# Three streamed cross-attentions: the query stack and the mask row move to ScalarE's DMA queue, and the rows of ones are copied from a row in memory

## The chip, the cores and the metric

The kernel runs on one core of one Trainium2 chip. The metric is device time in microseconds (us) of that core, from one launch that does the whole forward pass. A core has five engines with an instruction stream each: TensorE (PE; its weight loads are listed as PEld), VectorE (DVE), ScalarE (ACT), GpSimd (POOL) and SyncE (SP). Copies between memory (HBM) and the on-chip buffers are made by 16 DMA engines, which work off what the streams issue. In the kernel before, every one of the program's copies is issued by SP.

## The reference

A perceiver of four layers over 128 latent tokens of width 256. Each layer has a cross-attention to a context of 12544 keys of width 192, a self-attention of some kind, and a feed-forward network of eight experts. For layers 0 to 2 the cross-attention is, cut to what matters:

```python
q = split_heads(layernorm(x) @ Wq + bq)          # 16 heads of 16, 128 queries
k = split_heads(ctx @ Wk + bk)                   # 12544 keys
v = split_heads(ctx @ Wv + bv)
s = einsum('bhid,bhjd->bhij', q, k) / 4          # layer 0: keys outside the mask get -inf
x = x + merge(softmax(s) @ v) @ Wo + bo
```

## The kernel before, in words

`build` runs stages one after the other, each in a `Stage` with a barrier behind it: `setup`, `project_context`, then per layer a cross-attention, its output, a self-attention and the experts. `project_context` computes keys and values of layers 0 to 2 once; keys are written to memory (`key_parts`) as three bf16 parts whose sum is the fp32 key, values to `values_scratch`.

`streamed_cross_attention(layer)` (line 410) runs for layers 0, 1 and 2; in layer 1 it is called by `guarded_cross_attention`. Its fp32-like product of query and key is one matmul over stacked bf16 parts: rows 0 to 95 of the tile `keys` hold six copies of key parts of one head (6 times 16), and rows 0 to 95 of `q_stack` the query parts that go with them. Three further rows of `keys` (96 to 98) hold ones; opposite them in `q_stack` GpSimd later puts the negated maximum of each query in three parts. In layer 0 a fourth row, 99, holds the mask (0 or a very large negative number), with a row of ones opposite in `q_stack`.

The 16 heads are streamed. A head has 7 chunks of 1792 keys; `keys` and `values` have room for DEEP = 3 heads. `fill(h, j)` issues the copies of two chunks of a head (one chunk for j = 3): 48, 32 and 16 rows of keys (line 476) and the values (line 479), four copies in all; this text calls it a fill group. From head 3 on, a fill group waits until the sums of the chunks it overwrites are done. Per chunk, PE makes the scores with queries as rows (`top`, line 549), DVE reduces them to a maximum (line 697), and when a head's maximum is known and in `q_stack`, PE makes the scores again with keys as rows (`scores`, line 560), ACT takes exp (line 610) and PE sums probabilities times values (`sums`, line 573). `top` runs LEAD = 10 chunks ahead of `scores`, so that for the first 10 chunks `top` runs alone.

At the start of such a stage the order of SP's stream is written out by hand: Wq, bias or mask, the rows of ones into `keys` (line 489), the four fill groups of head 0; in layer 0 then a wait for the mask row computed by DVE (`drop_bf`), its copy to memory (`mask_row`, line 496), a wait for that, and three copies from there into row 99 (line 500); then a wait for the query parts (`qparts`, DVE, line 690), three copies of them to memory (`query_parts`, line 505), a wait for those, six copies back into `q_stack` (line 511, 16 rows of 16 times 128 each), in layer 0 one more for its row of ones (line 515); then the fill groups of heads 1 and 2 and of the rest. PE's first `top` waits for all rows of ones and mask (`key_rows`), the whole stack (`stack`) and the first fill group.

The source of the ones is `ones_bf`, a tile of 128 by 128; the copy into `keys` reads three of its rows 294 times over:

```python
sp.dma_start(keys[SEG:SEG + 3, :, :].rearrange("p s (n t) -> p (s n) t", t=128),
             g.ones_bf[0:3, :].unsqueeze(1).to_broadcast([3, RING * TPC, 128]))\
```

Of the kernel before, what the change touches and what calls it, by code (L numbers as in the profile page):

```python
# [149 lines left out]
def setup(nc, g, a):  # L150

    with ExitStack() as ctx:
        st = Stage(nc, ctx, "setup")
        block = st.block()

        @block.sync
        def _(sp):
            sp.dma_start(g.x[:], a["x"].rearrange("b t d -> (b t) d")).then_inc(st.sem("x"), 16)
            sp.wait_ge(st.sem("x"), 16)

        @block.gpsimd
        def _(pool):
            pool.memset(g.band[:], 0.0).then_inc(st.sem("zeroed"), 1)
            pool.memset(g.minus_half[:], -0.5)
            pool.memset(g.zeros[:], 0.0)
            pool.wait_ge(st.sem("zeroed"), 1)

            pool.affine_select(out=g.band[:], in_=g.band[:], compare_op=ALU.not_equal, fill=1.0, base=-127,
                               pattern=[[1, 255]], channel_multiplier=-1).then_inc(st.sem("band"), 1)

        @block.vector
        def _(dve):
            dve.memset(g.ones[:], 1.0)
            dve.memset(g.ones_bf[:], 1.0)
            dve.wait_ge(st.sem("band"), 1)
            dve.tensor_copy(g.ident_bf[:], g.ident)

            dve.tensor_copy(g.sel[:], g.ident[:, 0:32]).then_inc(st.sem("sel"), 1)
            dve.wait_ge(st.sem("sel"), 1)
            for i in range(1, 4):  # L180
                dve.tensor_tensor(g.sel[:], g.sel[:], g.ident[:, 32 * i:32 * i + 32], ALU.add)\
                   .then_inc(st.sem("sel"), 1)
                dve.wait_ge(st.sem("sel"), i + 1)
# [226 lines left out]
def streamed_cross_attention(layer):  # L410
# [18 lines left out]
    def stage(nc, g, a):  # L429
        with ExitStack() as ctx:  # L430
# [37 lines left out]
            def _(sp):  # L468
# [17 lines left out]
                          .then_inc(sem("wq"), 16)  # L486
                if masked:
                    sp.dma_start(mask8[:], a["mask"].rearrange("(p n) -> p n", p=128)).then_inc(sem("mask"), 16)
                sp.dma_start(keys[SEG:SEG + 3, :, :].rearrange("p s (n t) -> p (s n) t", t=128),
                             g.ones_bf[0:3, :].unsqueeze(1).to_broadcast([3, RING * TPC, 128]))\  # L490
                  .then_inc(sem("key_rows"), 16)
                for j in range(len(PAIRS)):
                    fill(0, j)
                if masked:
                    sp.wait_ge(sem("drop"), 1)
                    sp.dma_start(dram(g.mask_row, 0, [[NK // 128, 128], [1, NK // 128]]), drop_bf[:])\
                      .then_inc(sem("mask"), 16)
                    sp.wait_ge(sem("mask"), 32)
                    for p in range(DEEP):
                        sp.dma_start(keys[SEG + 3:SEG + 4, p * NCH:p * NCH + NCH, :],  # L500
                                     dram(g.mask_row, 0, [[NK, 1], [CH, NCH], [1, CH]])).then_inc(sem("key_rows"), 16)

                sp.wait_ge(sem("qparts"), 1)
                for part in range(3):
                    sp.dma_start(dram(g.query_parts, part * D * T, [[T, 128], [128 * T, DG], [1, T]]),
                                 qparts[:, part, :, :]).then_inc(sem("qparts_out"), 16)
                sp.wait_ge(sem("qparts_out"), 48)
                for at, copies in ((0, 3), (3, 2), (5, 1)):
                    for part in range(copies):
                        src = dram(g.query_parts, part * D * T, [[T, HD], [HD * T, H], [1, T]])  # L510
                        sp.dma_start(q_stack[at * HD + part:(at + copies) * HD:copies, :, :], src)\
                          .then_inc(sem("stack"), 16)
                if masked:
                    sp.wait_ge(sem("stack_zero"), 1)
                    sp.dma_start(q_stack[SEG + 3:SEG + 4, :, :],
                                 g.ones_bf[0:1, :].unsqueeze(1).to_broadcast([1, H, T]))\
                      .then_inc(sem("stack"), 16)
                for h in range(1, H):
                    for j, (c, n) in enumerate(PAIRS):
                        if h >= DEEP:  # L520
                            sp.wait_ge(sem("sums"), (h - DEEP) * NCH + c + n)
                        fill(h, j)

            @block.tensor
            def _(pe):
# [10 lines left out]
                    pe.matmul(bank(g, 2, 0, 1), g.ones[:], some[:], start=True, stop=True)\  # L536
                      .then_inc(sem("mask_count"), 1)
                pe.wait_ge(sem("stack"), STACK)
                pe.wait_ge(sem("key_rows"), 16 * (1 + DEEP) if masked else 16)
                pe.wait_ge(sem("q"), 1)  # L540

                def top(v, w):
# [10 lines left out]
                def scores(k):  # L553
                    h = (k * GROUP + GROUP - 1) // (NCH * TPC)
                    pe.wait_ge(sem("shifted"), 4 * (h + 1))
                    at_least(pe, sem("probs"), k - 2)
                    for i in range(GROUP):
                        tile = k * GROUP + i
                        u, key = tile // TPC, tile % TPC * 128
                        last = pe.matmul(score_bank(k)[:, i * 128:i * 128 + 128], keys[0:P2, u % RING, key:key + 128],  # L560
                                         q_stack[0:P2, u // NCH, :], start=True, stop=True, skip_group_check=True)
                    last.then_inc(sem("scores"), 1)
# [41 lines left out]

            @block.scalar
            def _(act):
                def exp(k):
                    act.wait_ge(sem("scores"), k + 1)
                    at_least(act, sem("sums"), -(-(k * GROUP + GROUP - HELD) // TPC))
                    act.activation(group_probs(k), score_bank(k), ACT.Exp).then_inc(sem("probs"), 1)  # L610

                def copy_tiles(h):
                    act.wait_ge(sem("sums"), NCH * (h + 1))
                    act.copy(tiles[:, h, :], sum_bank).then_inc(sem("tiles"), 1)

                for u in range(NU):
                    k = (u * TPC + GROUP // 2) // GROUP
                    exp(k)
                    exp(k + 1)
                    exp(k + 2)  # L620
                    if u % 2 == 0:
                        exp(k + 3)
                    if u % NCH == 0 and u > 0:
                        copy_tiles(u // NCH - 1)
                copy_tiles(H - 1)
# [2155 lines left out]
def build(nc, a, out, stages=None):  # L2781
    with ExitStack() as ctx:
# [18 lines left out]
        g.values = nc.dram_tensor("values_scratch", (3, H, NCH, 128, TPC * VW), F32, kind="Internal").ap()  # L2801
        g.query_parts = nc.dram_tensor("query_parts", (3, D, T), BF16, kind="Internal").ap()
        g.mask_row = nc.dram_tensor("mask_row", (1, NK), BF16, kind="Internal").ap()
        g.acc, g.neg_all = sb("acc", [T, H, VW]), sb("neg_all", [T, H])
        run = {name for name in ORDER} if stages is None else set(stages)
        setup(nc, g, a)
# [69 lines left out]
```

## Time and profile before

| | us |
|---|---|
| median of 3 runs | 3386.88 |
| the 3 runs | 3374.2, 3387.84, 3386.88 |
| the profiled execution, its own time | 3375.52 |
| its span, first to last instruction | 3373.8 |
| busy: PE / DVE / ACT / POOL | 2941.7 / 1829.3 / 1349.5 / 405.4 |
| mean granted TensorE clock, share of full | 0.906 |

Busy times are those of the span; an engine's busy time counts neither its waits nor the issuing of copies. What a stage costs beyond its busy time stands in the idle times before instructions and in what ended them.

### The profile page before, as it was taken

What the parts mean: (1) busy time and instruction counts of PE and PEld (TensorE: products, weight loads), DVE (VectorE), ACT (ScalarE), POOL (GpSimd) and SP (SyncE); (2) the same over time, 40 slices, a digit from 0 to 9 for tenths busy, and PEclk for the clock granted to TensorE, in tenths of its full rate; (3) what the DMA queues carried; (4) which work ended last, traced back from release to release, by engine and by line L of the source; (5) the groups of instructions that cost most, each with busy time, mean ns of one, the idle gap of its engine ahead of it and who ended that gap; (6) DMA issues with size and microseconds to landing.
All of it is one profiled execution on the core that took longest, in us unless ns stands there. A gap on an engine that the chain in (4) does not pass through costs nothing. (4 is left out here: it accounts for less than half of the span.)

```text
span 3373.8 us, 66493 instructions
## 1 busy us (share of the span) xinstructions
PE 2941.7 (87%) x27158; PEld 2484.3 (74%) x27158; DVE 1829.3 (54%) x3246; ACT 1349.5 (40%) x2191; POOL 405.4 (12%) x571
## 2 busy tenths in 40 slices
PE   6878829998677999576999669999999999999978
PEld 6878725776474777473777455999999999999867
DVE  5445427774426775455776343555555555555524
ACT  4444314666003667122667120444344344444311
POOL 2333310000100000000000002220202020200000
PEclk9989968999787999686999685999999999999969
DMA  4877868883468884059885271201101010000016
GB/s 154 266 259 253 274 190 184 177 175 62 154 192 179 174 177 88 26 204 181 177 175 103 83 213 38 57 11 29 39 1 39 1 39 1 1 1 1 17 50 227
DMA packets 244901, 393.95 MB, mean 117 GB/s; under 512 B 33491, under 2 KB 207957, under 8 KB 244597
## 3 DMA queue, kind: packets, MB, share of 16 engines
q1 hardware_dynamic: 244599, 389.70, 44.9%
q8 instruction: 217, 3.56, 0.5%
q14 instruction: 85, 0.69, 0.1%
HBM read 289.45 MB, written 99.49 MB: 115 GB/s over the span
## 5 line engine op out<-in xcount | busy, mean ns | idle before, releaser
L697 DVE TENSOR_REDUCE L_xattn_tops<-psum 128x1 f32<-128x896 f32 x672 | 702.1, 1086 | 264.8 <-PE psum L549 263.6
L610 ACT ACTIVATE L_xattn_probs<-psum 128x512 f32<-128x512 f32 x1176 | 612.0, 600 | 489.4 <-PE psum L560 489.3
L1705 DVE TENSOR_TENSOR L_units_low<-psum,L_units_high 128x896 fp32r<-128x896 f32 x224 | 243.6, 1088 | 486.7 <-ACT L_units_high L1654 486.7
L549 PE MATMUL psum<-L_xattn_keys,L_xattn_q_stack 96*128 96x448 bf16 (+1 forms) x1344 | 393.6, 377 | 109.0 <-DMA L_xattn_q_stack<-query_parts 64.5
L1622 PE MATMUL psum<-wide_tokens,L_units_high 128*128 128x386 f32 x1568 | 456.4, 358 | 1.4 <-DVE L_units_low L1705 1.4
L560 PEld LDWEIGHTS psum<-L_xattn_q_stack,L_xattn_keys 99*128 99x128 bf16 (+1 forms) x4704 | 321.4, 98 | 143.3 <-issue 17.4
L560 PE MATMUL psum<-L_xattn_q_stack,L_xattn_keys 99*128 99x128 bf16 (+1 forms) x4704 | 392.4, 221 | 5.0 <-ACT L_xattn_probs L610 5.0
L1623 PE MATMUL psum<-wide_tokens,L_units_low 128*128 128x194 f32 x1568 | 395.1, 252 | 0.0
L573 PE MATMUL psum<-L_xattn_probs,L_xattn_values 128*17 128x128 f32 x9408 | 357.1, 276 | 0.0
L1654 ACT CAST L_units_high<-psum 128x896 fp32r<-128x896 f32 x224 | 203.3, 908 | 363.6 <-PE psum L1610 363.6
L1646 ACT ACTIVATE L_units_raw<-L_units_raw,L_units_negmax 128x896 f32<-128x896 f32 x224 | 221.6, 1037 | 307.9 <-DVE L_units_negmax L1696 307.9
L1623 PEld LDWEIGHTS psum<-wide_tokens,L_units_low 128*128 128x128 f32 x1568 | 299.1, 191 | 1.7
L1622 PEld LDWEIGHTS psum<-wide_tokens,L_units_high 128*128 128x128 f32 x1568 | 294.9, 188 | 3.0 <-DVE L_units_low L1705 1.6
L573 PEld LDWEIGHTS psum<-L_xattn_probs,L_xattn_values 128*17 128x17 f32 x9408 | 260.1, 98 | 38.0 <-ACT L_xattn_probs L610 0.6
L1686 DVE TENSOR_SCALAR_CACHE_REDUCE L_units_raw<-psum 128x448 f32<-128x448 f32 x448 | 259.8, 617 | 4.0 <-POOL wide_acc L1665 2.6
L549 PEld LDWEIGHTS psum<-L_xattn_keys,L_xattn_q_stack 96*128 96x128 bf16 (+1 forms) x1344 | 91.4, 99 | 219.1 <-issue 67.1
L1610 PE MATMUL psum<-band,L_units_raw 128*128 128x128 f32 x1568 | 207.9, 272 | 2.0 <-ACT L_units_raw L1646 2.0
L395 POOL TENSOR_TENSOR proj_parts<-proj_rest,proj_parts 128x896 bf16<-128x896 f32 x84 | 161.6, 1925 | 280.0 <-ACT proj_parts L313 280.0
L1610 PEld LDWEIGHTS psum<-band,L_units_raw 128*128 128x128 f32 x1568 | 179.9, 140 | 10.3 <-ACT L_units_raw L1646 2.4
L1598 PE MATMUL psum<-wide_high_a,wide_q_high 128*128 128x448 f32 x448 | 184.5, 412 | 2.2 <-PEq L78 2.2
L2563 PE MATMUL psum<-xnT,L_ffn_w 128*128 128x128 f32 x1056 | 141.6, 292 | 27.3 <-DMA L_ffn_w<-in_L_ffn_W 14.0
L2563 PEld LDWEIGHTS psum<-xnT,L_ffn_w 128*128 128x128 f32 x1056 | 137.3, 206 | 36.0 <-issue 14.0
(436 smaller groups left out, 3990.3 us busy)
## 6 DMA issues: line engine op xcount, KB each, us to landing
key_parts<-proj_parts SPq DMA_DIRECT2D x84, 672.0 KB, 4.1
L_xattn_keys<-key_parts SPq DMA_DIRECT2D x144, 336.0 KB, 4.7
values_scratch<-proj_values SPq DMA_DIRECT2D x21, 1904.0 KB, 17.4
L_xattn_values<-values_scratch SPq DMA_DIRECT2D x144, 238.0 KB, 5.2
L_ffn_w<-in_L_ffn_W SPq DMA_DIRECT2D x32, 1024.0 KB, 6.9
L_xattn_keys<-key_parts SPq DMA_DIRECT2D x144, 224.0 KB, 5.0
L_xattn_keys<-key_parts SPq DMA_DIRECT2D x192, 112.0 KB, 5.0
L_ffn_w<-in_L_ffn_w SPq DMA_DIRECT2D x16, 1024.0 KB, 6.4
```

The costliest lines, as they stand in the source:

```text
L549: last = pe.matmul(top_slot(n)[:, s, :], q_stack[0:P1, h, :], keys[0:P1, v % RING, key:key + WIN // 2], start=True, stop=True)
L560: last = pe.matmul(score_bank(k)[:, i * 128:i * 128 + 128], keys[0:P2, u % RING, key:key + 128], q_stack[0:P2, u // NCH, :], start=True, s ...
L573: last = pe.matmul(sum_bank[row:row + VW, :], values[:, u % RING, t, :], probs[:, at:at + 128], start=(c * TPC + t < 4), stop=(c * TPC + t ...
L610: act.activation(group_probs(k), score_bank(k), ACT.Exp).then_inc(sem("probs"), 1)
L697: dve.tensor_reduce(tops[:, h % 2, 2 * c + w:2 * c + w + 1], top_slot(n), AX.XY, ALU.max)\
L1610: last = pe.transpose(turned_banks(gr)[:, t * 128:t * 128 + 128], raw[u % 2][:, key:key + 128], g.ident)
L1622: pe.matmul(out, high[gr][:, cols], rhs, start=(tile == 0), stop=False, skip_group_check=True)
L1623: last = pe.matmul(out[:, 0:C + 2], low[gr][:, cols], rhs[:, 0:C + 2], start=False, stop=(tile == TPC - 1), skip_group_check=True)
L1646: act.activation(half, half, ACT.Exp, bias=new).then_inc(sem("probs"), 1)
L1686: dve.tensor_scalar(raw[u % 2][:, s * SUB:s * SUB + width], bank(g, s % 2, 0, width), 0.0, None, ALU.add, ALU.max, accum_out=tops[:, h, s: ...
L1705: dve.tensor_tensor(low[gr][:], turned_banks(gr), high[gr][:], ALU.subtract).then_inc(sem("low"), 1)
L2563: last = pe.matmul(bank(g, 2 * slot + half, j * T, j * T + T), buf[par][:, k, col:col + 128], g.xnT[:, k, :], start=(k == 0), stop=(k == D ...
```

## The change

In `setup`, one further copy writes the tile of ones to a new row in memory, `ones_row` of 12544 values. In the streamed attention, SP issues only Wq, bias or mask, and then all fill groups, head 0 to 15. ACT, before its first exp, issues the rows of ones (from `ones_row`, 3 times 21 pieces of 1792 values), in layer 0 the whole mask path and the stack's row of ones, then one copy of all query parts to memory instead of three, and the same six copies into `q_stack`. PE's wait for the rows of ones moves from the first `top` to the first `scores` in layers 1 and 2, and stays where it was in layer 0 (where the first `scores` waits too).

```diff
@@ setup @@
             sp.dma_start(g.x[:], a["x"].rearrange("b t d -> (b t) d")).then_inc(st.sem("x"), 16)
-            sp.wait_ge(st.sem("x"), 16)
+            sp.wait_ge(st.sem("ones_bf"), 1)
+            sp.dma_start(dram(g.ones_row, 0, [[128, NK // 128], [1, 128]]), g.ones_bf[0:NK // 128, :])\
+              .then_inc(st.sem("x"), 16)
+            sp.wait_ge(st.sem("x"), 32)
...
-            dve.memset(g.ones_bf[:], 1.0)
+            dve.memset(g.ones_bf[:], 1.0).then_inc(st.sem("ones_bf"), 1)
@@ streamed_cross_attention, sync @@
-                sp.dma_start(keys[SEG:SEG + 3, :, :].rearrange("p s (n t) -> p (s n) t", t=128),
-                             g.ones_bf[0:3, :].unsqueeze(1).to_broadcast([3, RING * TPC, 128]))\
-                  .then_inc(sem("key_rows"), 16)
-                for j in range(len(PAIRS)):
-                    fill(0, j)
-                if masked:
-                    sp.wait_ge(sem("drop"), 1)
...
-                sp.wait_ge(sem("qparts"), 1)
-                for part in range(3):
-                    sp.dma_start(dram(g.query_parts, part * D * T, [[T, 128], [128 * T, DG], [1, T]]),
-                                 qparts[:, part, :, :]).then_inc(sem("qparts_out"), 16)
-                sp.wait_ge(sem("qparts_out"), 48)
...
-                for h in range(1, H):
+                for h in range(H):
@@ tensor @@
-                pe.wait_ge(sem("key_rows"), 16 * (1 + DEEP) if masked else 16)
+                if masked:
+                    pe.wait_ge(sem("key_rows"), 16 * (1 + DEEP))
...
                 def scores(k):
                     h = (k * GROUP + GROUP - 1) // (NCH * TPC)
                     pe.wait_ge(sem("shifted"), 4 * (h + 1))
+                    if k == 0:
+                        pe.wait_ge(sem("key_rows"), 16 * (1 + DEEP) if masked else 16)
@@ scalar @@
+                act.dma_start(keys[SEG:SEG + 3, :, :], dram(g.ones_row, 0, [[0, 3], [0, RING], [1, CH]]))\
+                   .then_inc(sem("key_rows"), 16)
+                if masked:
+                    act.wait_ge(sem("drop"), 1)
+                    act.dma_start(dram(g.mask_row, 0, [[NK // 128, 128], [1, NK // 128]]), drop_bf[:])\
+                       .then_inc(sem("mask"), 16)
+                    act.wait_ge(sem("mask"), 32)
+                    for p in range(DEEP):
+                        act.dma_start(keys[SEG + 3:SEG + 4, p * NCH:p * NCH + NCH, :],
+                                      dram(g.mask_row, 0, [[NK, 1], [CH, NCH], [1, CH]])).then_inc(sem("key_rows"), 16)
+                    act.wait_ge(sem("stack_zero"), 1)
+                    act.dma_start(q_stack[SEG + 3:SEG + 4, :, :],
+                                  g.ones_bf[0:1, :].unsqueeze(1).to_broadcast([1, H, T]))\
+                       .then_inc(sem("stack"), 16)
+
+                act.wait_ge(sem("qparts"), 1)
+                act.dma_start(dram(g.query_parts, 0, [[T, 128], [D * T, 3], [128 * T, DG], [1, T]]), qparts[:])\
+                   .then_inc(sem("qparts_out"), 16)
+                act.wait_ge(sem("qparts_out"), 16)
+                for at, copies in ((0, 3), (3, 2), (5, 1)):
+                    for part in range(copies):
+                        src = dram(g.query_parts, part * D * T, [[T, HD], [HD * T, H], [1, T]])
+                        act.dma_start(q_stack[at * HD + part:(at + copies) * HD:copies, :, :], src)\
+                           .then_inc(sem("stack"), 16)
```

SP's stream before, at the start of layer 1's streamed attention (each fill group is four rows; the middle of head 0 is left out):

```order
L482 DMA L_xattn_wq<-in_L_xattn_Wq 128x2x256
L485 DMA L_xattn_bq<-in_L_xattn_bq 128x1 x2
L489 DMA L_xattn_keys<-ones_bf 3x294x128
L476 DMA L_xattn_keys<-key_parts 48x1x3584
...
L476 DMA L_xattn_keys<-key_parts 16x1792
L479 DMA L_xattn_values<-values_scratch 128x238
L505 DMA query_parts<-L_xattn_qparts 128x2x128 x3
L511 DMA L_xattn_q_stack<-query_parts 16x16x128 x6
L476 DMA L_xattn_keys<-key_parts 48x1x3584
```

The same place of SP's stream in the changed kernel (line numbers are its own, 3 higher here):

```order
L485 DMA L_xattn_wq<-in_L_xattn_Wq 128x2x256
L488 DMA L_xattn_bq<-in_L_xattn_bq 128x1 x2
L479 DMA L_xattn_keys<-key_parts 48x1x3584
...
L479 DMA L_xattn_keys<-key_parts 16x1792
L482 DMA L_xattn_values<-values_scratch 128x238
L479 DMA L_xattn_keys<-key_parts 48x1x3584
```

The ones and the query copies are gone from it, and head 1's first fill group follows head 0's last. ACT's stream in the changed kernel at the start of layer 0's streamed attention; before, the exps (line 610 then) were its first rows there:

```order
L584 DMA L_xattn_keys<-ones_row 3x21x1792
L588 DMA mask_row<-L_xattn_drop_bf 128x98
L592 DMA L_xattn_keys<-mask_row 1x12544 x3
L595 DMA L_xattn_q_stack<-ones_bf 1x16x128
L600 DMA query_parts<-L_xattn_qparts 128x6x128
L606 DMA L_xattn_q_stack<-query_parts 16x16x128 x6
L612 ACTIVATE L_xattn_probs<-psum 128x512 x28
```

In layers 1 and 2 the rows of lines 588, 592 and 595 are absent. The copies stand ahead of all exps of the stage, in the order in which they are needed.

## Rows read from the trace of the kernel before

**Rows 1.** Page: costliest groups, the one that carries the first wait.

```profile
L549 PE MATMUL psum<-L_xattn_keys,L_xattn_q_stack 96*128 96x448 bf16 (+1 forms) x1344 | 393.6, 377 | 109.0 <-DMA L_xattn_q_stack<-query_parts 64.5
```

**Rows 2.** Tile q_stack: who waited for it (engine, line: us, times).

```profile
  PEld psum L549: 100.0, 3
```

**Rows 3.** Timeline, layer 0's start: start us, us, engine, line, copy [idle before].

```profile
469.20 0.97 SPq L489 DMA_DIRECT2D L_xattn_keys<-ones_bf  x1
...
475.86 0.27 DVE L677 TENSOR_SCALAR L_xattn_drop_bf<-L_xattn_drop,L_xattn_any_key 128x98 bf16<-128x98 f32 x1
...
490.51 0.34 SPq L496 DMA_DIRECT2D mask_row<-L_xattn_drop_bf  x1
498.55 0.82 SPq L500 DMA_DIRECT2D L_xattn_keys<-mask_row  x3
499.42 1.41 SPq L505 DMA_DIRECT2D query_parts<-L_xattn_qparts  x3
504.43 3.85 SPq L511 DMA_DIRECT2D L_xattn_q_stack<-query_parts  x6
508.32 0.59 SPq L515 DMA_DIRECT2D L_xattn_q_stack<-ones_bf  x1
...
510.23 1.67 PE L549 MATMUL psum<-L_xattn_keys,L_xattn_q_stack 100*128 100x448 bf16 x4 [34.85 <-DMA L_xattn_q_stack<-ones_bf]
...
511.20 14.97 DVE L697 TENSOR_REDUCE L_xattn_tops<-psum 128x1 f32<-128x896 f32 x14 [32.15 <-PE psum L549]
```

**Rows 4.** Timeline, layer 1's start.

```profile
992.70 0.84 SPq L489 DMA_DIRECT2D L_xattn_keys<-ones_bf  x1
...
993.59 12.46 SPq L476 DMA_DIRECT2D L_xattn_keys<-key_parts  x3
...
998.72 0.43 DVE L690 TENSOR_TENSOR L_xattn_qparts<-L_xattn_qrest,L_xattn_qparts 128x256 bf16<-128x256 f32 x1
...
1006.55 1.84 SPq L476 DMA_DIRECT2D L_xattn_keys<-key_parts  x3
1008.43 0.42 SPq L479 DMA_DIRECT2D L_xattn_values<-values_scratch  x1
...
1013.57 1.46 SPq L505 DMA_DIRECT2D query_parts<-L_xattn_qparts  x3
1023.73 3.87 SPq L511 DMA_DIRECT2D L_xattn_q_stack<-query_parts  x6
...
1029.40 1.67 PE L549 MATMUL psum<-L_xattn_keys,L_xattn_q_stack 96*128 96x448 bf16 x4 [32.61 <-DMA L_xattn_q_stack<-query_parts]
```

**Rows 5.** Timeline, layer 2's start.

```profile
1514.27 0.42 DVE L690 TENSOR_TENSOR L_xattn_qparts<-L_xattn_qrest,L_xattn_qparts 128x256 bf16<-128x256 f32 x1
...
1544.20 1.67 PE L549 MATMUL psum<-L_xattn_keys,L_xattn_q_stack 96*128 96x448 bf16 x4 [31.86 <-DMA L_xattn_q_stack<-query_parts]
```

**Rows 6.** Windows: stretch, its us, busy by engine, PEclk, DMA share, GB/s.

```profile
994.00:996.00 2.00, 1.28 (x6) 1.28 (x7) 0.43 (x1) 0.00 (x0) 0.00 (x0) 0.50 0.18 18
1000.00:1002.00 2.00, 0.00 (x0) 0.00 (x0) 0.00 (x0) 0.00 (x0) 0.00 (x0) 0.50 0.16 19
504.40:508.30 3.90, 0.00 (x0) 0.00 (x0) 0.00 (x0) 0.00 (x0) 0.00 (x0) 0.50 0.30 67
514.00:530.00 16.00, 13.55 (x31) 2.00 (x30) 15.62 (x17) 0.00 (x0) 0.77 (x4) 0.50 1.06 207
```

**Rows 7.** DMA view, 499 to 504 us: GB/s in 40 equal slices.

```profile
GB/s 0 0 0 201 0 0 0 0 0 0 47 219 189 37 33 213 193 254 20 201 209 62 0 0 0 0 0 201 0 0 0 0 0 0 0 18 16 18 16 18
```

**Rows 8.** Page: issues by copy, KB each, median us to landing.

```profile
L_xattn_keys<-key_parts SPq DMA_DIRECT2D x144, 336.0 KB, 4.7
L_xattn_values<-values_scratch SPq DMA_DIRECT2D x144, 238.0 KB, 5.2
L_xattn_keys<-key_parts SPq DMA_DIRECT2D x144, 224.0 KB, 5.0
L_xattn_keys<-key_parts SPq DMA_DIRECT2D x192, 112.0 KB, 5.0
```

**Rows 9.** Tile query_parts, copies out and back: us to landing.

```profile
DMA to landing us min/median/max: 2.0/2.4/9.3
```

**Rows 10.** Timeline, the first 4 us: setup and the next stage's first copy.

```profile
0.81 0.41 SPq L158 DMA_DIRECT2D x<-in_x  x1
...
1.06 0.17 DVE L174 MEMSET ones_bf<- 128x128 bf16 x1
```

More of the change, by code:

```diff
@@ L488, in _ @@
                     sp.dma_start(mask8[:], a["mask"].rearrange("(p n) -> p n", p=128)).then_inc(sem("mask"), 16)
-                sp.dma_start(keys[SEG:SEG + 3, :, :].rearrange("p s (n t) -> p (s n) t", t=128),
-                             g.ones_bf[0:3, :].unsqueeze(1).to_broadcast([3, RING * TPC, 128]))\
-                  .then_inc(sem("key_rows"), 16)
-                for j in range(len(PAIRS)):
-                    fill(0, j)
-                if masked:
-                    sp.wait_ge(sem("drop"), 1)
[L496 to L501, printed above, removed]
-                sp.wait_ge(sem("qparts"), 1)
-                for part in range(3):
-                    sp.dma_start(dram(g.query_parts, part * D * T, [[T, 128], [128 * T, DG], [1, T]]),
-                                 qparts[:, part, :, :]).then_inc(sem("qparts_out"), 16)
-                sp.wait_ge(sem("qparts_out"), 48)
[L508 to L517, printed above, removed]
-                for h in range(1, H):
+                for h in range(H):
                     for j, (c, n) in enumerate(PAIRS):
@@ L2803, in build @@
         g.mask_row = nc.dram_tensor("mask_row", (1, NK), BF16, kind="Internal").ap()
+        g.ones_row = nc.dram_tensor("ones_row", (1, NK), BF16, kind="Internal").ap()
         g.acc, g.neg_all = sb("acc", [T, H, VW]), sb("neg_all", [T, H])
```

## The prediction

> **What bounds the kernel now.** I read the page's costliest groups first: TensorE's first score matmul of the streamed attention stood idle for copies, 64.5 us of it for the query stack [rows 1]. The view of the tile q_stack gives the whole: 100.0 us in 3 waits, one at the start of each of layers 0, 1 and 2 [rows 2]. That is 3% of the span and all that this change can reach, since behind the first matmul nothing of the program differs.
>
> The timelines of the three starts show what fills such a wait. Take layer 1 [rows 4]. SP issues the ones at 992.70. The next issue, three copies that cost 1.84 us elsewhere, takes 12.46: the queue is held. The windows say by what: 19 GB/s with 0.16 of the DMA engines busy, that is 2.6 engines of 16 [rows 6]; 3 times 294 pieces of 256 bytes crawl through three engines. Meanwhile the query parts are done at 998.72 + 0.43 = 999.15 us, but their copy is issued at 1013.57, behind head 0's four fill groups. It lands late, behind their data: the six copies into the stack start at 1023.73, and TensorE at 1029.40. So 30.3 us pass between the query and its use, and two issues and their landings in a quiet queue would need about 8. Layer 2 is the same: 1514.69 to 1544.20, 29.5 us [rows 5]. In layer 0 the chain begins with the mask: drop is done at 476.13, its copy is issued at 490.51, the copies back wait until 498.55, the query's round trip takes 499.42 to 504.43, and TensorE starts at 510.23, 34.1 us after drop [rows 3]. No engine computes anything behind that wait; time taken from it should come off the span one for one.
>
> **The change part by part.**
>
> *Setup.* One copy more, issued when `ones_bf` is there (1.06 + 0.17 = 1.23 us), where x was issued by 1.22 [rows 10]. It lands about 0.4 us behind x; it costs 0.4 us, between 0 (hidden by the other engines) and 2.0, the smallest time to landing [rows 9].
>
> *The ones.* From 882 pieces of 256 bytes to 63 of 3584 bytes. The source's first dimension is still 3, so I take it that 3 engines still carry it: 75 KB each. Two prices: a single engine moved the mask rows at 17 GB/s [rows 7], so 4.4 us; in the loaded stretch 207 GB/s over 16 engines is 12.9 GB/s each [rows 6], so 5.8 us. Either replaces about 12 us in which the whole queue stood. What covers it: it is needed by the first `scores` in layers 1 and 2, and by the first `top` in layer 0, both later than about 480 + 10 us. On the path it costs nothing, unless the query's rows queue behind it on these three engines; issued at about 993, alone 4.4 us and shared 8.8, it is gone by 1002, before the query's copy needs the same ring much. Uncovered it would cost up to 3 us per layer.
>
> *Fills.* They start where the ones were, with a group (336 + 224 + 112 + 238 KB [rows 8]) every 4.5 us at 207 GB/s [rows 6], though SP can issue one in 1.84 + 0.42 = 2.3 us [rows 4]. Head 0 is 3.5 groups, 15.8 us, plus 5.8 on the three engines. `top` takes 2.14 us per chunk (14 reductions in 14.97 us [rows 3]), 4.3 us per group, so it needs group j at its start + 4.3 j. Starting no earlier than 14 us after the first fill, it is never short of keys by more than a microsecond. SP now issues 12 groups in a row instead of 4 before the query copies: this is the new competitor, priced next.
>
> *Query and mask on ACT's queue.* The trace before has no two loaded queues at once, so I bound the price. Low end, as in a quiet queue: a copy out is 0.5 us of issue + 2.0 to landing [rows 9], the stack 1029.40 − 1023.73 = 5.7 us [rows 4]. Then TensorE starts in layer 1 at 999.15 + 2.5 + 5.7 = 1007.3 (22.1 us earlier), in layer 2 at 1522.9 (21.3), in layer 0 after 476.13 + 2.3 (mask out) + 0.82 + 0.59 (issues) + 5.0 − 0.9 (the round trip, two issues fewer) + 5.8 at 489.7 (20.5). Together 63.9 us.
>
> What I take: on each engine, every copy of ACT waits one turn of a copy of SP. A fill group is four copies in 4.5 us, so a turn is 1.1 us; the copy's own work is small (0.30 of 3.9 us for six, 0.2 us each [rows 6]). The merged query copy is as large as three and gets 3 turns. Layer 1: out at 999.15 + 2.5 + 3.4 = 1005.0; the stack is 0.6 for the first issue, 6 turns of 1.3 = 7.8, and 1.8 to land = 10.2; start 1015.3, **14.1 us earlier**. Layer 2: 1514.69 + 5.9 + 10.2 = 1530.8, **13.4 earlier**. Layer 0: mask out 476.13 + 2.3 + 1.1 = 479.5, issues to 480.9; the three mask rows crawl on one engine at 17 GB/s [rows 7], 75 KB, 4.4 us alone and 8.8 when every other turn is SP's, to 489.2; behind them on that engine the query copy, 3.4 + 2.0, to 494.6; stack to 504.8, **5.4 earlier**. The sum is 32.9 − 0.4 = 32.5 us. I take this and not the quiet end because the DMA engines are shown full while fills run, 207 GB/s at a busy share of 1.06 [rows 6].
>
> *What does not change.* ACT's issues (six at 0.65 us) lie before its first exp, at least 21 us after the first `top`. The granted clock is already at 0.50 (1.2 GHz) 2 us after the fill starts, during TensorE's own small matmuls [rows 6]; a wait of 17 instead of 33 us finds it there too, and VectorE, not TensorE, paces the lone `top`s (15.62 of 16 us busy [rows 6]). From head 3 on, fills wait for sums as before.
>
> **The base.** The profiled execution took 3375.5 us, span 3373.8. The three runs are 3374.2, 3386.9 and 3387.8; the median is 11.4 us above the profiled one, and that difference I can't place in the trace. From the median: 3386.9 − 32.5 = **3354.4 us**; from the profiled run 3343.0.
>
> **The rivals.**
>
> 1. *Quiet queue.* ACT's few small rows pass nearly unhindered: −63.9 + 0.4, 3323.4 us. For it: small copies in their own queue. Against: full engines [rows 6].
>
> 2. *The wait moves.* ACT's copies are slowed to where under 17 us is left, for instance 4 us per layer; 3375 us. It takes about 2.0 instead of 1.1 us per turn (9 turns, 8 us more per layer). For it: layer 0's chain of three round trips.
>
> 3. *Row by row, slower.* If an engine alternates between queues after each row and not after each copy, a small row of ACT pays for a large one of SP. A group has 96/16 = 6 key rows and 256/16 = 16 value rows per engine, 22 in 4.5 us, 0.2 us a row; query out and stack are 48 + 96 = 144 rows per engine, 144 × 0.21 = 30 us, plus 4.5 of issues and landings. Layer 1 then starts at about 1034 (+4.5), layer 2 at 1549 (+5), layer 0 at about 518 (+8): +18, 3405 us. It decides once a row's turn costs over 0.17 us: from there on the wait is longer than before.
>
> 4. *One line, slower.* If the engines serve copies in order of issue whatever the queue, the stack lies behind what SP has issued ahead. At 2.3 us a group, nearly all 10.5 groups of three heads are issued by 1019 and need 47 us: start at about 1044, +15, in each layer: +42, 3429 us. It decides when more than 7 groups lie ahead of the stack. For it: in the trace the query copy took up to 9.3 us to land behind four groups [rows 9]. Against: that was one queue, and order within one queue says nothing of two.
>
> The Trainium skill ("DMA: Bandwidth & Descriptors", section "Issuing engines are not separate DMA queues") speaks against this change: copies from SP, ACT and GpSimd run on the same 16 engines and interleave, and issuing from several engines saves only the issue time. Read strictly that is rival 4, or at best rival 2: by it the sum would be a loss of 42 or a gain under 17 us. No row before has two queues, so the trace doesn't decide. Another section of that page ("Queues, rings and completion order") says that each queue has its own ring on each engine and that the engine changes rings after a packet, typically 9 to 17 descriptors; by it a turn is about a copy's share, which gives my sum and not rival 3. No run here shows it yet.
>
> **How the numbers follow.** A measurement of this kernel can tell 0.5% from no change, 17 us: faster is below 3370, slower above 3404. Forecast 0.62 (gains of 17 to 50 us), quiet queue 0.16, the wait moves 0.11, row by row 0.06, one line 0.05. Faster 0.62 + 0.16 = 0.78, same 0.11, slower 0.06 + 0.05 = 0.11. The range reaches down past the quiet queue to 3320, since the base may be the lower one, and up to 3376, into rival 2. Left out are rivals 3 and 4, a third of rival 2, and a little below: about 0.18.
>
> **What would show it.** Right: the issue of 12.46 us becomes about 1.8; a second hardware queue with some 1 MB; the first `top` about 23 us after the first fill issue in layer 1, 35 in layer 0; no new wait behind it; the ones no longer on the path; the three waits of 100 us sum to about 67. Rivals 3 and 4: query and stack copies taking 10 us and more to land, and the first `top` later than 37 us after the stage's start. Wrong in another way: a `top` or `scores` waiting for a fill or for the ones, or a stage elsewhere that became longer.

## The result, and the profile after

The changed kernel takes 3444.1 us (median of 4 runs, 3441.5 to 3455.3) against 3387.0 before: a ratio of 1.018, 95% interval 1.0162 to 1.0198. It is 57 us slower. The forecast was 3354.4, 32.5 us faster. The profiled execution took 3443.8 us, its span is 3442.0, 68.2 more than before; the mean granted clock is 0.899 instead of 0.906.

The page of the changed kernel: the busy times barely move, a second hardware queue (q10, ACT's) carries 2.55 MB, and the wait of the first score matmul has grown.

```profile
PE 2942.7 (85%) x27158; PEld 2484.8 (72%) x27158; DVE 1829.6 (53%) x3246; ACT 1349.7 (39%) x2191; POOL 405.4 (12%) x571
...
q10 hardware_dynamic: 7628, 2.55, 0.6%
...
L524 PE MATMUL psum<-L_xattn_keys,L_xattn_q_stack 96*128 96x448 bf16 (+1 forms) x1344 | 394.3, 378 | 145.3 <-DMA L_xattn_q_stack<-query_parts 135.7
```

The tile q_stack of the changed kernel says the same as [rows 2], where it was 100.0 us:

```profile
  PEld psum L524: 136.3, 3
```

That is 36 us more. The rest of the loss is ahead of it in the same stages. The timeline of layer 1's start (compare [rows 4]):

```profile
1019.14 0.38 SPq L485 DMA_DIRECT2D L_xattn_wq<-in_L_xattn_Wq  x1
1019.16 0.27 ACTq L584 DMA_DIRECT2D L_xattn_keys<-ones_row  x1
...
1020.55 1.87 SPq L479 DMA_DIRECT2D L_xattn_keys<-key_parts  x3
...
1033.98 5.23 SPq L479 DMA_DIRECT2D L_xattn_keys<-key_parts  x3
...
1035.03 0.74 DVE L683 TENSOR_SCALAR L_xattn_q<-psum,L_xattn_bq 128x128 f32<-128x128 f32 x2 [12.72 <-PE psum L505]
...
1037.37 0.39 ACTq L600 DMA_DIRECT2D query_parts<-L_xattn_qparts  x1
...
1053.35 4.16 ACTq L606 DMA_DIRECT2D L_xattn_q_stack<-query_parts  x6
...
1078.41 1.68 PE L524 MATMUL psum<-L_xattn_keys,L_xattn_q_stack 96*128 96x448 bf16 x4 [43.42 <-DMA L_xattn_q_stack<-query_parts]
```

The stage loses in three places. Everything is counted from the issue of Wq (1019.14 here, 991.30 before). The query parts are ready to be copied out at 18.2 us instead of 7.9. Their copy takes 16.0 us to land. The stack takes 25.1 us from first issue to first `top`. Together 59.3 us, where the kernel before took 38.1 and the forecast had 24. The stall of 12.46 us on SP is gone, as intended. But the wait that TensorE's projection of the query now shows is new:

```profile
PEld psum L505 <- DMA L_xattn_bq<-in_L_xattn_bq: 22.6, 2, 11.5
```

It waits 11 us for Wq and the bias in each of layers 1 and 2 (for Wq, 9.5, in layer 0), where before it was 2.8 us for all three together. The first `top` moved from 42.0, 38.1 and 37.2 us to 63.9, 59.3 and 59.4: 65.3 us later in all, of a span that grew by 68.2.

The view of the queues, in the 16 us of the copy out and in the 26 us behind it (columns: packets, MB, share of 16 engines):

```profile
q1 hardware_dynamic: 1519, 3.19, 100.0%
q10 hardware_dynamic: 784, 0.20, 8.8%
...
q1 hardware_dynamic: 2250, 4.47, 84.5%
q10 hardware_dynamic: 1632, 0.39, 12.7%
```

SP's fills take the engines whole. While 0.20 MB of the query go out, 3.19 MB of keys and values come in. By the order of issue nearly all of them are of heads 1 and 2, and head 1 is needed only seven chunks, some 15 us, behind the first `top`.

### The profile page after: what moved, and what is told of

It reads as the page before. It is cut to its first block and busy times, and to the rows that moved or that the text cites. A ratio compares the mean times of both kernels' runs of the same rounds, so it can differ in the third digit from the quotient of the medians.

```text
span 3442.0 us, 66489 instructions
## 1 busy us (share of the span) xinstructions
PE 2942.7 (85%) x27158; PEld 2484.8 (72%) x27158; DVE 1829.6 (53%) x3246; ACT 1349.7 (39%) x2191; POOL 405.4 (12%) x571
## 3 DMA queue, kind: packets, MB, share of 16 engines
q10 hardware_dynamic: 7628, 2.55, 0.6%
## 5 line engine op out<-in xcount | busy, mean ns | idle before, releaser
L699 DVE TENSOR_REDUCE L_xattn_tops<-psum 128x1 f32<-128x896 f32 x672 | 702.3, 1086 | 301.9 <-PE psum L524 300.7
L2565 PE MATMUL psum<-xnT,L_ffn_w 128*128 128x128 f32 x1056 | 141.7, 292 | 26.4 <-DMA L_ffn_w<-in_L_ffn_W 13.5
L1601 PE MATMUL psum<-wide_low_a,wide_q_high 128*128 128x448 f32 x448 | 163.9, 366 | 0.0
```

The source lines that it names most:

```text
L699: dve.tensor_reduce(tops[:, h % 2, 2 * c + w:2 * c + w + 1], top_slot(n), AX.XY, ALU.max)\
```

## The experiments

All are compared with the kernel before on the same chip, in runs of the same batch. They ran on four chips, on which the kernel before took 3400 us (e1 to e4), 3401 (e5 to e8), 3382 (e9, e10) and 3383 (e11, e12), so differences of medians and ratios are read here, not times. Two landmarks of each profile, counted from the issue of Wq, in layers 0, 1 and 2:

| kernel | first top | first exp | time against before | ratio, 95% interval |
|---|---|---|---|---|
| before | 42.0, 38.1, 37.2 | 64.9, 61.0, 60.1 | | |
| the change | 63.9, 59.3, 59.4 | 86.8, 82.1, 82.2 | +57 | 1.0162 to 1.0198 |
| e1 hold heads 1 and 2 | 36.6, 32.6, 33.0 | 59.5, 55.5, 55.9 | −15 | 0.9942 to 0.9971 |
| e2 ones after Wq | 62.6, 54.9, 56.6 | 85.5, 77.8, 79.5 | +57 | 1.0142 to 1.0176 |
| e3 long rows | 63.8, 56.1, 55.1 | 86.7, 79.0, 78.0 | +52 | 1.0143 to 1.0177 |
| e4 ones row only | 38.6, 34.1, 33.6 | 61.5, 57.0, 56.5 | −14 | 0.9943 to 0.9971 |
| e5 two groups, ACT | 30.2, 19.5, 20.0 | 53.4, 48.8, 49.5 | −27 | 0.9897 to 0.9930 |
| e6 two groups, SP | 32.1, 19.4, 19.6 | 55.0, 49.1, 48.8 | −25 | 0.9911 to 0.9945 |
| e7 split, two groups | 29.4, 19.2, 18.9 | 52.2, 50.0, 49.6 | −33 | 0.9875 to 0.9914 |
| e8 split, one group | 27.0, 15.2, 14.8 | 49.9, 50.5, 50.6 | −34 | 0.9881 to 0.9914 |
| e9 memset, one group | 26.2, 27.7, 27.5 | 49.0, 53.2, 51.9 | −16 | 0.9927 to 0.9967 |
| e10 memset, two groups | 31.6, 27.4, 27.4 | 54.4, 50.2, 50.3 | −21 | 0.9907 to 0.9955 |
| e11 late memset, two | 31.4, 18.6, 18.9 | 54.3, 41.5, 41.8 | −42 | 0.9854 to 0.9887 |
| e12 late memset, one | 26.4, 15.2, 15.2 | 49.3, 40.4, 40.2 | −44 | 0.9849 to 0.9894 |

### e1: hold the fills of heads 1 and 2

My theory: the engines alternate between the two queues, and what ACT's copies meet is the eight fill groups that SP used to issue behind the stack. The rival: ACT's queue is slow by itself.

```diff
                 for h in range(H):
+                    if h == 1:
+                        sp.wait_ge(sem("stack"), STACK)
                     for j, (c, n) in enumerate(PAIRS):
```

> The changed kernel, with one wait more on SP: the fills of head 1 and later are issued only when the query stack has landed. Theory (an ACT row waits for an SP row on each DMA engine, and the eight fill groups of heads 1 and 2 that SP now issues ahead are what it meets): up to the query parts nothing changes (18.2 us from the stage's start in layer 1), by then head 0 has nearly landed, the round trip takes 6 to 8 us instead of 16.0 and the stack 6 to 8 instead of 25.1; the first top comes 31 to 34 us after the start instead of 59.3, some 75 us in all off 3444: 3365 to 3375 us, faster than before by 10 to 20. Rival (ACT's own queue is slow to issue or to land by itself, whatever SP does): the copies stay at 16 and 25 us, 3444.

ACT's stream and TensorE's first `top` in layer 1:

```profile
1006.75 0.27 ACTq L586 DMA_DIRECT2D L_xattn_keys<-ones_row  x1
1024.76 0.39 ACTq L602 DMA_DIRECT2D query_parts<-L_xattn_qparts  x1
1033.55 3.91 ACTq L608 DMA_DIRECT2D L_xattn_q_stack<-query_parts  x6
...
1039.34 1.68 PE L526 MATMUL psum<-L_xattn_keys,L_xattn_q_stack 96*128 96x448 bf16 x4 [16.96 <-DMA L_xattn_q_stack<-query_parts]
```

The copy out takes 8.8 us instead of 16.0 and the stack 5.8 instead of 25.1, the same as in the quiet queue before (5.7). The times to landing of all copies into the stack, in the three layers, fall from a median of 14.1 us in the changed kernel to 2.5 (view of the tile q_stack of e1):

```profile
DMA to landing us min/median/max: 2.3/2.5/4.3
```

One wait turns +57 into −15. ACT's queue is not slow; it is slow beside SP's fills. The query parts are still late, 18.0 us, as expected.

### e2: the ones behind Wq

The theory for the late Wq: the ones, issued by ACT at the same moment, share three engines with it. In the view of the queues of the changed kernel, 1021 to 1033 us, their rows are heavy:

```profile
q10 hardware_dynamic: 58, 0.20, 12.1%
```

58 rows of 3584 bytes take 12.1% of 16 engines for 12 us, 0.40 us each; 21 of them per engine are 8.4 us. By the theory Wq's 16 rows there alternate with them. The rival: SP's own fills, behind Wq, delay its landing.

```diff
+                act.wait_ge(sem("wq"), 16 * (3 if biased else 1))
                 act.dma_start(keys[SEG:SEG + 3, :, :], dram(g.ones_row, 0, [[0, 3], [0, RING], [1, CH]]))\
                    .then_inc(sem("key_rows"), 16)
```

> The changed kernel, with ACT's copy of the ones issued only when Wq and the bias have landed. Theory (Wq and bias land 13 us late because on three engines their rows alternate with the 21 rows of 3584 bytes that ACT issued at the same time): Wq and bias land in 3 us, the query parts are ready 8 us after the start in layer 1 instead of 18.2, the copies behind are as slow as before, 40 us, first top at 49 to 52 instead of 59.3: 3415 to 3423 us. Rival (it is SP's own fills behind them that delay the landing of Wq and bias): the query stays at 18 us or later, 3444.

Layer 1 of its trace:

```profile
1038.87 2.07 PE L505 MATMUL psum<-xnT,L_xattn_wq 128*128 128x128 f32 x8 [0.70 <-DMA L_xattn_bq<-in_L_xattn_bq]
...
1043.32 0.42 ACTq L601 DMA_DIRECT2D query_parts<-L_xattn_qparts  x1
1062.96 4.34 ACTq L607 DMA_DIRECT2D L_xattn_q_stack<-query_parts  x6
```

The wait is 0.70 us instead of 11; the copy out is issued at 7.9 us instead of 18.2. The theory for Wq holds, the fills were innocent of that. But the 10 us are mostly given back: the copy out lands in 19.6 us, the stack takes 27.4, and the first `top` comes at 54.9, 4.4 us earlier in layer 1 and not 7 to 10. The 21 to 29 us expected in time did not come: the gain cannot be told from nothing (+57 against before, on another chip than the change's +57). I read it so that an earlier start into a full queue meets more fills; that was not tried apart.

### e3: fewer rows for the same bytes

Which law do the engines follow? Rows 2048 elements long leave the bytes and the number of copies alone and cut the rows of the stack from 96 to 6 per engine.

```diff
+                for part in range(3):
+                    for k in range(DG):
+                        act.dma_start(dram(g.query_parts, part * D * T + k * 8 * T, [[T, 8], [H * T, HD], [1, T]]),
+                                      qparts[:, part, k, :]).then_inc(sem("qparts_out"), 16)
+                act.wait_ge(sem("qparts_out"), 96)
...
-                        src = dram(g.query_parts, part * D * T, [[T, HD], [HD * T, H], [1, T]])
+                        src = dram(g.query_parts, part * D * T, [[H * T, HD], [1, H * T]])
```

> The changed kernel, with query_parts laid out in memory so that a row of the stack is one piece of 4096 bytes instead of 16 of 256: each engine gets 6 rows for the stack instead of 96, for the same bytes. The copy out takes six issues on 8 engines, 96 rows on each instead of 48 on each of 16. Theory row by row: the stack takes 6 to 9 us instead of 25.1 (the issue of six copies and landing), the copy out 22 to 30 instead of 16.0; together 8 to 12 us less per layer, 3408 to 3420 us. Rival one line (order of issue decides, all copies wait for the bytes ahead): the stack stays at 20 us or more. Rival turn per copy: the stack stays about the same too, since it is six copies as before.

```profile
1047.17 3.94 ACTq L602 DMA_DIRECT2D query_parts<-L_xattn_qparts  x6
1073.06 3.79 ACTq L609 DMA_DIRECT2D L_xattn_q_stack<-query_parts  x6
...
1085.20 1.68 PE L524 MATMUL psum<-L_xattn_keys,L_xattn_q_stack 96*128 96x448 bf16 x4 [40.42 <-DMA L_xattn_q_stack<-query_parts]
```

The stack takes 12.1 us instead of 25.1 and the copy out, 96 rows on each of what I take to be 8 engines, 25.9 instead of 16.0. For the stack, bytes and number of copies are the same and SP's fills still fill the engines (a share of 0.92 or more in every 2 us from 1073 to 1085), so a turn per copy, at a fixed price, falls: the rows decide. For the copy out that isn't separated, since it went from one copy to six as well. The forecast of time was missed: together 38.0 us instead of 41.1 in layer 1, and +52 us where 21 to 33 over the kernel before were expected.

One line falls too. SP's last copies before the stack, and the stack itself, in the view of DMA issues (1069 to 1073 us, 1073 to 1086 us; us to landing last):

```profile
L_xattn_values<-values_scratch SPq DMA_DIRECT2D x1, 238.0 KB, 19.3
...
L_xattn_q_stack<-query_parts ACTq DMA_DIRECT2D x6, 64.0 KB, 8.8
```

SP issued these values at 1068.94 and they landed at 1088.2; the stack, issued from 1073.06 on, had landed by 1085.2. It overtook them.

But it is not rows alone. A stack copy of one row per engine still took 8.8 us to land, where row by row would give 3. As an estimate, 8.6 us + 0.17 per row comes within 1 us of the three: 1 row (8.8 us), 48 rows (16.0) and 96 rows (25.9, from the first of six issues to the last landing); quiet copies of 16 rows landed in 2.3 to 2.5. So beside a full queue a trip pays some 6 us once, and 0.17 us per row, near the 0.2 us that a fill's row takes. The first of the six, with nothing of ACT's ahead of it, took 9.1 us, so the 6 us are not the six waiting for each other. What they are (rows of SP that an engine has already taken in, perhaps) was not tried apart and stays open.

### e4: the ones alone

```diff
-                sp.dma_start(keys[SEG:SEG + 3, :, :].rearrange("p s (n t) -> p (s n) t", t=128),
-                             g.ones_bf[0:3, :].unsqueeze(1).to_broadcast([3, RING * TPC, 128]))\
+                sp.dma_start(keys[SEG:SEG + 3, :, :], dram(g.ones_row, 0, [[0, 3], [0, RING], [1, CH]]))\
                   .then_inc(sem("key_rows"), 16)
```

(and the row itself, written in `setup`; all else is the kernel before)

> The kernel before with one part of the change alone: the ones come from the row in memory (63 pieces of 3584 bytes instead of 882 of 256), still first on SP's queue, and nothing moves to ACT. Theory: the issue of 12.46 us becomes about 2, the three engines are held 4 to 6 us instead of 12, everything behind shifts by 6 to 8 us in each of the three layers: 3363 to 3369 us. Rival (the 12 us were hidden behind something else, or the three engines stay held as long): 3387 within 5.

SP's stream in layer 1:

```profile
1009.03 0.31 SPq L492 DMA_DIRECT2D L_xattn_keys<-ones_row  x1
1009.38 1.87 SPq L479 DMA_DIRECT2D L_xattn_keys<-key_parts  x3
...
1018.90 8.81 SPq L507 DMA_DIRECT2D query_parts<-L_xattn_qparts  x3
1035.88 3.87 SPq L513 DMA_DIRECT2D L_xattn_q_stack<-query_parts  x6
```

The stall behind the ones is gone, and over half of it comes back behind the four fill groups: the query copies now take 8.81 us to issue instead of 1.46. They are issued 11.3 us after the stage's start instead of 22.3, and take 17.0 us to land instead of 10.2. The first `top` is 3.4 to 4.0 us earlier per layer, not 6 to 8; −14 us in all, not 18 to 24. This half of the change is a gain by itself. It also shows that one queue is no refuge: the 17.0 us of the copy out are as long as its 16.0 on ACT's queue in the changed kernel.

### e5 and e6: two groups ahead, on ACT's queue and on SP's

If the order is what counts, SP should issue only as many fills as it can move before the query is ready, and then wait for the stack. The two kernels have the same order; one keeps mask, query and stack on ACT's queue, the other issues all of it from SP.

```diff
                     for j, (c, n) in enumerate(PAIRS):
+                        if h == 0 and j == 2:
+                            sp.wait_ge(sem("stack"), STACK)
```

> Query, mask and stack on ACT's queue as in the change, but SP issues only the first two fill groups of head 0 and waits for the stack before the others; the ones are issued once Wq has landed (layer 0) or behind the stack (layers 1 and 2). Theory (a copy on ACT's queue costs its quiet time plus some 6.5 us and 0.17 us per row and engine only while SP's fills run): query parts at 8 us after the start in layers 1 and 2, copy out 6 to 9, stack 5.8, first top at 20 to 24 instead of 38 in the kernel before; layer 0 at 26 to 29 instead of 42. In all 40 to 50 us less than the kernel before. Rival (moving to ACT's queue costs something by itself): less than 25 us.

> The same order with everything on SP's queue: two fill groups, then mask and query, then the ones (layer 0: the ones first), then the other fills. Nothing is on ACT's queue. Theory (the gain is in the order, not in the second queue; in one queue the copy out follows the two groups, which have landed by 12 us): first top at 18 to 22 in layers 1 and 2 and 27 to 30 in layer 0; within 8 us of the two-group version on ACT, 40 to 52 us less than the kernel before. Rival (the second queue is what makes the query early): 20 us slower than the ACT version or more.

First `top` at 19.5 and 19.4 us in layer 1; −27 and −25 us, inside each other's intervals. So in this order, where SP issues nothing beside the query's copies, the second queue gives nothing that this measurement can tell. Both are better than before and still below the 40 to 52 expected: in e5 47 us of earlier first `top` became 27 of time. The first exp tells most of it: it moved by 34 us in all, not 47. The tops run out of keys: between first `top` and first exp TensorE stands 10 us in each of layers 1 and 2, where before it was 3.

The rest is behind the first exp. In the 60 us behind it TensorE never stood still in the kernel before, in the change or in e1 to e3, and 1.2 us in e4; in e5 to e12 it stood 10.7, 7.5, 3.4, 4.9, 10.4, 6.0, 6.1 and 8.7 us, the three layers together. The longest such stop of e5, in layer 1:

```profile
1071.56 0.22 PE L539 MATMUL psum<-L_xattn_q_stack,L_xattn_keys 99*128 99x128 bf16 x1
1075.71 0.91 PE L539 MATMUL psum<-L_xattn_q_stack,L_xattn_keys 99*128 99x128 bf16 x7 [3.93 <-issue]
```

It stands between matmuls of one group of `scores`, between which the program waits for nothing, and the profile names no releaser. The DMA engines are full there (a share of 1.06). What the stop is stays open.

### e7 and e8: the stack shared by both queues, two groups or one

```diff
+                        if h == 0 and j == 1:
+                            sp.wait_ge(sem("qparts_out"), 16)
+                            stack_copies(sp, (3, 2), (5, 1))
```

(ACT issues the other three copies, and in layer 0 the query copy ahead of the mask rows; j is 2 in e7)

> As the two-group version on ACT, with three of the six stack copies issued by SP at the same time, fills let go right behind them, and in layer 0 the query copy issued ahead of the mask rows. Theory: the six issues of 0.65 us are shared, 2 us less in each layer, and 4 more in layer 0: 48 to 58 us less than the kernel before. Rival (fills let go too early slow the ACT half of the stack by its rows): no better than the version that waits for the stack.

> As the split version, with one fill group ahead of the query instead of two. Theory: the copy out is quiet (2.5 to 4 us), first top at 14 to 17 in layers 1 and 2, 17 to 20 in layer 0, 55 to 66 us less than the kernel before, with a stall of under 3 us per layer behind the first top. Rival (the fills now come too late, and the tops wait for them): the first top is as early, but waits for fills behind it give back more than 5 us per layer, 50 us less or worse than the two-group version.

−33 and −34 us: both missed (48 to 58 and 55 to 66), and the rival of e8 was right. Against e5 the split is 7 us better, within the intervals. The first `top` is 4 us earlier than with two groups, the first exp is not. TensorE in layer 1 of e8:

```profile
1016.98 1.93 PE L534 MATMUL psum<-L_xattn_keys,L_xattn_q_stack 96*128 96x448 bf16 x4 [0.44 <-DVE L_xattn_tops L711]
1029.38 1.67 PE L534 MATMUL psum<-L_xattn_keys,L_xattn_q_stack 96*128 96x448 bf16 x4 [10.47 <-DMA L_xattn_values<-values_scratch]
```

After one group the tops stand 10.5 us for the second, issued 17 us earlier. Beside it, from 1012.24 on, run the ones on ACT's queue.

### e9 and e10: the ones without a copy

GpSimd (11 of 21 chunks) and ScalarE (10) write the ones of layers 1 and 2 while they would idle.

```diff
+                if not masked:
+                    pool.memset(keys[SEG:SEG + 3, 0:HALF, :], 1.0).then_inc(sem("pool_ones"), 1)
+                    pool.wait_ge(sem("pool_ones"), 1)
```

> As the split version with one fill group ahead, but in layers 1 and 2 the rows of ones are written by GpSimd (11 of 21 chunks) and ScalarE (10), which idle there, instead of by a copy; layer 0 keeps the copy. Theory (once the stack is early, the tops wait for fills, and on three engines the fills lie behind 75 KB of ones each, 4 to 6 us): the first exp comes at 44 to 47 us in layers 1 and 2 instead of 50.5, 8 to 12 us less than the split version with one group, 42 to 46 less than the kernel before. Rival (the fills' own bytes set the first exp, the ones do not matter): no change, 34 less than the kernel before.

> The same with two fill groups ahead of the query. Theory: the engines are busier during the query's round trip, so the fills are further on: first exp at 42 to 46 us in layers 1 and 2, 42 to 50 less than the kernel before. Rival (no difference between one and two groups, as in the two split versions): within 3 us of the one-group version.

Both missed: −16 and −21 us. The first `top` in layer 1 came at 27.4 us (e10) instead of 19.2 (e7). VectorE and GpSimd in e10:

```profile
991.00 16.52 POOL L659 MEMSET L_xattn_keys<- 3x19712 bf16 x1
...
995.15 12.52 DVE L710 CAST L_xattn_qparts<-L_xattn_q 128x256 bf16<-128x256 f32 x1
1007.71 0.42 DVE L712 TENSOR_TENSOR L_xattn_qrest<-L_xattn_q,L_xattn_qparts 128x256 f32<-128x256 f32 x1
```

A cast of 0.29 us takes 12.52 and ends when the memset does, at 1007.5. This explains the late first `top`, but not why the time is 12 to 18 us behind that of e7 and e8: over the three layers the first exps are only 3 us later. The stops behind them are 3 to 6 us longer, the chip is another one, and the rest stays open.

### e11 and e12: the memset after the cast

```diff
                 if not masked:
+                    pool.wait_ge(sem("sums_zero"), 1)
                     pool.memset(keys[SEG:SEG + 3, 0:HALF, :], 1.0).then_inc(sem("pool_ones"), 1)
```

> The memset version with two groups, GpSimd's memset waiting until VectorE has finished the query parts. In the version before, one VectorE cast of the query parts took 12.5 us instead of 0.29 and ended when GpSimd's memset did. Theory (the two exclude each other on SBUF-to-SBUF work, and VectorE's reductions from PSUM are not held): the cast takes 0.3 us, query parts at 8 us, first top at 19 to 21 in layers 1 and 2 instead of 28, first exp at 43 to 47 instead of 50; 10 us less than the version before, 30 to 38 less than the kernel before. Rival (the reductions of the first tops are held too): the tops stretch behind the first one by 5 us or more, nothing gained.

> The same with one fill group ahead of the query. Theory: first top at 15 to 17 in layers 1 and 2, waits for fills behind it 2 us each at most, first exp at 42 to 46; within 4 us of the two-group version. Rival (too few fills ahead): first exp at 48 or later, as in the split version with one group.

```profile
994.33 0.29 DVE L711 CAST L_xattn_qparts<-L_xattn_q 128x256 bf16<-128x256 f32 x1
...
1007.37 12.79 DVE L722 TENSOR_REDUCE L_xattn_tops<-psum 128x1 f32<-128x896 f32 x12 [11.20 <-PE psum L535]
...
996.30 16.52 POOL L660 MEMSET L_xattn_keys<- 3x19712 bf16 x1 [6.46 <-DVE psum L717]
```

The cast is back at 0.29 us, and the reductions from PSUM run at 1.07 us each (12 in 12.79 us), those beside the memset, up to 1012.8, like the others. The first exp comes at 40 to 42 us in layers 1 and 2, 8 to 10 earlier than in e7 and e8, and the time is 3340.8 and 3339.4 us against 3383.3: −42 and −44, ratios 0.9871 (0.9854 to 0.9887) and 0.9872 (0.9849 to 0.9894). That is more than the 30 to 38 expected. These two beat both the kernel before and the change; the rival for e12 fell. Of the 48 and 56 us by which the first exps are earlier over the three layers, 6.1 and 8.7 are lost in stops behind them. Against e7 the intervals of the ratio overlap a little: that the ones without a copy bring the first exp forward is clear, that they save time over e7 is not clear of noise.

## Why the prediction was wrong

*What bounds the kernel.* Right. The three waits were the place, and no stage elsewhere changed by much: 65.3 of 68.2 us of span are the later first tops. "One for one" held for the change and for e1 (15.1 us of earlier first tops, −15 us), but not where the first tops came 31 to 61 us earlier in all (e5 to e12): there TensorE stands again behind them.

*The ones.* I wrote that on the path they cost nothing unless the query's rows queue behind them, and looked only at the query. Wrong: they took the three engines from Wq and the bias, which are issued in the same microsecond. That made the query parts some 10 us later in layer 1 (e2 gives them back). Before, the ones were issued after Wq in one queue, and TensorE waited only 2.8 us for Wq and bias in three layers. A DMA moved to another queue must be compared with everything that is in flight there, the small loads ahead of it too.

*Query and mask on ACT's queue.* This is the step that failed most: "on each engine, every copy of ACT waits one turn of a copy of SP", 1.1 us each. The copy out was to take 5.9 us and took 16.0, the stack 10.2 and took 25.1. In layer 0 the mask's copy to memory was to take 3.4 us and took 11.9. The price grows with the rows: by the estimate from e3, 0.17 us for each of 48 + 96 rows (24 us), and some 6 us more for each of the two trips through full engines. Rival 3, with 0.2 us a row and 34.5 us for the two, was nearest in mechanism and had 0.06; measured were 41.1. It lacked the fixed part, and it lacked the late Wq, so its +18 became +57. Rival 4, with +42, was nearer in the number, but by luck: e3 shows the stack overtaking copies issued before it.

The page of the Trainium skill that I weighed ("DMA: Bandwidth & Descriptors", "Queues, rings and completion order") has the engine change rings after a packet, typically 9 to 17 descriptors. I took it that by this a turn is a copy's share, 1.1 us. That was wrong on my own figures: a copy of SP has 1 to 16 rows per engine, 5.5 in the mean, and 9 to 17 rows at 0.2 us would be, as an estimate from the page's figure, 1.8 to 3.4 us a turn. With nine turns that takes back 6 to 21 of the 14 us of layer 1. The runs don't tell such turns from turns of one row: if both queues give about 16 rows a turn, a long copy of ACT also pays about one fill's row for each of its own. The other rule ("Issuing engines are not separate DMA queues": several issuing engines save only the issue time) agrees with e5 against e6, −27 against −25 us. Read as that, it should have had a greater chance than the 0.16 that I gave rivals 2 and 4 together.

*Fills.* The sentence that SP "now issues 12 groups in a row instead of 4 before the query copies: this is the new competitor" was right, and e1 shows its size: held back, the same kernel is 15 us faster than before instead of 57 slower. The old order was not only slow; it also kept the queue short while the query went through (its copy out landed in 10.2 us, against 17.0 in e4 without the stall).

*Setup.* 0.4 us was fair: layer 0's stage starts at 468.54 instead of 468.25, 0.3 us later.

*Range and chances.* 3320 to 3376 left out both slower rivals, with 0.11 between them. Both ends of the price of a copy under load rested on a trace without one loaded second queue. I took the middle as if I knew it. The rows that bounded it (engines at a share of 1.06) spoke for the slow end.

## What to carry to other kernels

A second DMA queue does not give a small, urgent copy a way past large ones: on full engines it pays for every row, and what helps is to issue less ahead of it. Few and long rows made the stack faster (e3), but not the kernel by more than the noise. Before streaming far ahead, hold back what is not needed yet until the critical round trip is through. And follow the gain to the next gate: here the first `top` could be made 23 us earlier, but time followed the first exp, which needs the keys of ten chunks; it stopped at 49 to 51 us in layers 1 and 2 (e5 to e8) until the ones no longer used the same engines. Then TensorE's stops behind the first exp took back a part.

## What the runs showed of the hardware that I had not expected

A GpSimd memset of 3 by 19712 bf16 values (16.52 us) held a VectorE cast of 128 by 256 values from SBUF to SBUF for 12.52 us instead of 0.29 (e10), while VectorE's scaling from PSUM (0.74 us for two, as ever; e10) and its reductions from PSUM (1.07 us; e11) ran beside it at full pace. And SP's queue fills up: once some groups are ahead, an issue that takes 1.46 us takes 8.81 (e4), and three key copies of 1.84 take up to 7.99 in the changed kernel.
